# Attention probabilities turned by DVE in 32x32 blocks instead of by PE, and a product with V in four 32-row groups of the PE array

## The reference

```python
scale = DIM_HEAD ** (-0.5)                      # 16 heads of 64
xn = layer_norm(x, ln_g, ln_b)                  # x: (32, 112, 256)
cn = layer_norm(context, cln_g, cln_b)          # context: (32, 375, 256)
q = (xn @ Wq).reshape(b, n, HEADS, DIM_HEAD).transpose(0, 2, 1, 3) * scale
k, v = jnp.split(cn @ Wkv, 2, axis=-1)          # one k and one v for all heads
sim = jnp.einsum('bhid,bjd->bhij', q, k) + mask[:, None, :, :]
attn = jax.nn.softmax(sim, axis=-1)
out = jnp.einsum('bhij,bjd->bhid', attn, v)
out = out.transpose(0, 2, 1, 3).reshape(b, n, INNER) @ Wout
val, gate = jnp.split(xn @ W1, 2, axis=-1)
out = out + jax.nn.silu(gate) * val @ W2
```

## Time and profile before

| | |
|---|---|
| median of 3 runs | 1851.41 us (1844.26 to 1853.59) |
| span of the profiled execution, first to last instruction | 1848.1 us |
| PE matmul busy | 1761.8 us, 95% of the span |
| DVE busy | 1310.7 us, 71% |
| ACT busy | 918.7 us, 50% |
| POOL busy | 420.3 us, 23% |
| groups 1 to 6, each | 149.7 us |

### The profile page before, as it was taken

How to read it: one execution, slowest core, us unless ns; L and a number is a source line. 1 busy time by engine, 2 the same in 40 slices (tenths; PEclk the granted TensorE clock), 3 DMA queues, 4 the chain that set the end, 5 groups by cost and what they waited for, 6 DMA issues and landing times.

```text
span 1848.1 us, 27947 instructions
## 1 busy us (share of the span) xinstructions
PE 1761.8 (95%) x9224; PEld 1020.1 (55%) x9224; DVE 1310.7 (71%) x3971; ACT 918.7 (50%) x2262; POOL 420.3 (23%) x569
## 2 busy tenths in 40 slices
PE   4579999999999998999999999999999999999997
PEld 2356676766767544455545554544555554555466
DVE  6878988988976588476667648747747666765744
ACT  3444553553541465456545545645645654654542
POOL 4868677777872001000000000000000000000000
PEclk8689999999999999999999999999999999999999
DMA  4000000000013343232222222323223322232200
GB/s 132 11 11 11 21 21 11 31 21 27 6 39 111 95 138 103 55 79 73 73 67 72 76 71 65 81 57 80 66 64 79 75 70 68 72 82 58 54 19 21
DMA packets 102318, 109.22 MB, mean 59 GB/s; under 512 B 38592, under 2 KB 95872, under 8 KB 101280
## 3 DMA queue, kind: packets, MB, share of 16 engines
q1 hardware_dynamic: 101712, 106.99, 21.7%
q10 hardware_dynamic: 464, 0.46, 0.1%
HBM read 96.92 MB, written 7.42 MB: 56 GB/s over the span
## 4 chain that ended last, share of the span: by engine, by line
PE 86%; DVE 8%; ACT 2%; DMA 2%; issue 1%; POOL 1%; DVEq 0%; POOLq 0%; ACTq 0%
PE ps L1530 20%; PE ps L1485 9%; PE ps L1492 9%; PE ps L1523 9%; PE ps L1508 8%; PE ps L314 5%; PE ps L440 4%; PE ps L387 4%; PE ps L427 4%; PE ps L405 3%; PE ps L1590 2%; DVE m_u L727 2%; PE ps L373 2%; PE ps L1584 1%; PE ps L1628 1%
## 5 line engine op out<-in xcount | busy, mean ns | idle before, releaser
L1867 DVE CUSTOM_DVE_ANT_0 x_pr<-ps,x_mk 128x375 f32<-128x375 f32 x448 | 227.6, 545 | 306.1 <-issue 238.9
L1739 ACT ACTIVATE x_pT<-ps 125x384 f32<-125x384 f32 x448 | 195.5, 489 | 269.8 <-PE ps L1492 269.2
L1745 ACT ACTIVATE x_pr<-x_pr,x_mx 128x375 f32<-128x375 f32 x448 | 268.2, 608 | 30.4 <-DVE x_mx L1867 30.4
L1492 PEld LDWEIGHTS ps<-ident,x_pr 128*125 128x125 f32 x1344 | 164.5, 187 | 130.9 <-issue 95.7
L1492 PE MATMUL ps<-ident,x_pr 128*125 128x128 f32 x1344 | 205.7, 289 | 2.5 <-DVE x_pr L1876 2.5
L1530 PE MATMUL ps<-x_xn,x_w 128*128 128x448 f32 x512 | 205.7, 543 | 2.1 <-DVE x_ff L1927 2.1
L1485 PE MATMUL ps<-x_kT,x_qT 64*128 64x375 f32 x896 | 202.6, 529 | 4.1 <-DVE x_mx L1867 4.1
L1876 DVE TENSOR_SCALAR x_pr<-x_pr,x_rc 128x375 f32<-128x375 f32 x448 | 170.9, 424 | 8.0
L1508 PE MATMUL ps<-x_pT,x_va 125*64 125x512 f32 (+1 forms) x768 | 158.4, 548 | 0.6 <-ACT x_pT L1739 0.6
L314 PE MATMUL ps<-m_xa,w_in 128*128 128x448 f32 x352 | 148.2, 568 | 6.2 <-ACT m_xa L532 6.2
L1485 PEld LDWEIGHTS ps<-x_kT,x_qT 64*128 64x128 f32 x896 | 67.7, 185 | 126.3 <-issue 114.4
(11 more groups left out here) (195 smaller groups left out, 2867.3 us busy)
## 6 DMA issues: line engine op xcount, KB each, us to landing
x_mk<-in_mask SPq DMA_DIRECT2D x224, 187.5 KB, 2.4
x_cx<-in_context SPq DMA_DIRECT2D x32, 375.0 KB
x_cT<-in_context_turned SPq DMA_DIRECT2D x32, 375.0 KB, 3.3
x_rb<-context_roots SPq DMA_DIRECT2D x32, 187.5 KB, 4.9
m_Rd<-bc_roots SPq DMA_DIRECT2D x8, 448.0 KB, 3.6
x_mixed<-m_x SPq DMA_DIRECT2D x8, 448.0 KB, 4.0
X<-x_mixed SPq DMA_DIRECT2D x8, 448.0 KB, 4.9
m_X<-in_x SPq DMA_DIRECT2D x7, 448.0 KB, 4.0
```

The costliest lines, as they stand in the source:

```text
L1492: last = pe.transpose(bank(2 + e)[0:JP, t * ROWS:(t + 1) * ROWS], pr[:, 2 * (p % SLOT) + e, t * JP:(t + 1) * JP], ident[:, :])
L1739: act.activation(pT[:, 2 * NV * (batch(p) % 2) + 2 * (p % NP % NV) + e, :, :].rearrange("p t s -> p (t s)"), bank(2 + e)[0:JP, 0:JT * ROWS ...
L1745: act.activation(pr[:, k, :], pr[:, k, :], ACT.Exp, scale=-1.0, bias=mx[:, k:k + 1], accum_out=sums[:, k:k + 1]).then_inc(h_e.sem, 1)
L1867: dve.tensor_tensor_reduce(pr[:, k + e, :], bank(e)[:, 0:J], mk[:, p % SLOT, :], -1.0, 3.0e38, ALU.add, ALU.min, mx[:, k + e:k + e + 1]).t ...
```

## The change

The probabilities are no longer turned by PE. ACT now multiplies them by the reciprocal (`scaled`, in the step after `exps`), DVE turns them within blocks of 32x32 (`turn`, one instruction of 128x384 for each e) into a ring of nine places (`blocks`), and DVE's reciprocal (`divide`) moves to the end of its own step. ACT's two `copies` out of PSUM go. Each block row of 32 partitions then holds other query rows for the same 32 keys, so the product with V is done in four groups of 32 rows of the array at once, each with its own copy of V (`va` has V four times; still eight DMAs for a batch, each with four times as many pieces of 128 bytes) and into its own PSUM bank (2, 3, 4 and 5). A batch takes 12 key blocks x 4 row groups x 2 values of e = 96 matmuls of 224 columns, in two halves at steps 1 and 2 of the next batch, between the slots X and Y, and four copies in `heads_out` at step 3. Since four banks go to this product, the filler pieces have two seats, banks 6 and 7, in place of three, and the table of pieces is laid out anew. The table also decides when the norms run. Some buffers are shared (`so` in place of `so`, `x2` and `fs`), and the last group's end uses other banks.

```diff
-NV = 4
-NB = 2
 SLOT = 4
-MISC = (6, 7, 5)
+MISC = (6, 7)
 SEATS = len(MISC)
 XB = 2
-RESULT, TOKENS, TOKENS_FIRST, FINAL = (10, 11, 12), (20, 21, 22), (16, 17, 20), {STEPS - 2: (0,), STEPS - 1: (1, 2)}
+RESULT, TOKENS, TOKENS_FIRST, FINAL = (11, 12, 13), (17, 20, 23), (16, 17, 20), {STEPS - 2: (0,), STEPS - 1: (1, 2)}
+BLK = 32
+RB = ROWS // BLK
+JC = 12
+JW = JC * BLK
+AHEAD_BY = 2
+RING = NP + AHEAD_BY
+V_AT, V_TAKEN = (1, 2), 3
+V_BANKS = (2, 3, 4, 5)
+UP_BANKS = (0, 2, 3, 4)
 CONTEXT = (0, 1, 4)
-VPARTS = DH // 32 * (ROWS // 32)
+VPARTS = RB * DH // BLK
...
-    for c in range(KD):
-        for n in range(4):
-            at[4 * c + n + (1 if c or n >= 2 else 0), "Y"].append(("out", c, n))
+    for n in range(QUERIES, KA):
+        at[n - QUERIES, "X"].append(("query", n))
+    for n, p in enumerate(OUT_AT):
+        at[p, "Y"].append(("out", n // KA, n % KA))
     for n, s in enumerate("XY"):
-        at[9, s].append(("back", n))
+        at[11, s].append(("back", n))
+        at[17, s].append(("ftoken", n))
+        at[25 + n, "Y"].append(("down", n))
+        at[25, s].append(("token", n))
     for f in range(KH):
-        at[W1_AT + f, "X"].append(("gate", f))
-        at[W1_AT + f, "Y"].append(("value", f))
-    for n, s in enumerate("XY"):
-        at[18, s].append(("ftoken", n))
-        at[24, s].append(("token", n))
-        at[25, s].append(("down", n))
+        at[GATE_AT[f], "X"].append(("gate", f))
+        at[VALUE_AT[f], "Y"].append(("value", f))
     for n in range(KH):
-        at[20 + n // 2, "XY"[n % 2]].append(("up", n))
+        at[UP_AT[n], "Y"].append(("up", n))
     for b in range(GB):
         at[(b - 1) % GB * NP + NP - 2, "X"].insert(0, ("kv", b))
-    at[STEPS - 1, "Y"] += [("query", n) for n in range(QUERIES)]
-    for n in range(QUERIES, KA):
-        at[n - QUERIES, "X"].append(("query", n))
+    for n in range(QUERIES):
+        at[STEPS - 1 - (n == 0), "Y"].append(("query", n))
...
+OUT_AT = (0, 0, 3, 3, 4, 5, 5, 6, 6, 7, 7, 7, 8, 9, 10, 10)
+GATE_AT, VALUE_AT = (11, 12, 13, 14, 15, 17, 19, 20), (11, 12, 13, 14, 16, 17, 19, 20)
+UP_AT = (18, 18, 21, 21, 22, 23, 24, 24)
...
         return int(piece[0] == "value")
     if piece[0] == "out":
-        return 2
-    if piece[0] == "kv":
-        return 2 if piece[1] != 1 else 0
+        return 1 - piece[1]
+    if piece[0] == "kv" or piece[0] == "query" and piece[1] >= QUERIES:
+        return 0
     return piece[-1] % 2
...
-    pT = sb("x_pT", [JP, 2 * 2 * NV, JT, ROWS])
+    blocks = sb("x_blk", [ROWS, RING, 2, JC, BLK])
...
+    def tile_of(p):
+
+        b, n = divmod(p, NP)
+        return (n + NP - AHEAD_BY * (b % 2)) % NP
+
+    def place_of(p):
+
+        return tile_of(p) + AHEAD_BY * (p // NP % 2)
...
-        def values_in(i, b):
+        def values(i, b):
+
             sp.wait_ge(c_t.sem, c_t.value(i, b + 1))
-            hold(sp, h_o, i, NB * (b - 1))
-            for k in range(DH // 32):
-                for q in range(ROWS // 32):
-                    n = min(32, JP - 32 * q)
-                    sp.dma_start(va[32 * q:32 * q + n, b % 2, :, 32 * k:32 * k + 32], vT[32 * k:32 * k + n, :, 32 * q:32 * q + 32]).then_inc(l_va[b % 2].sem, 16)
+            hold(sp, h_o, i, b - 1)
+            for a in range(RB):
+                for k in range(DH // BLK):
+                    sp.dma_start(va[BLK * a:BLK * a + BLK, b % 2, :, BLK * k:BLK * k + BLK],
+                                 vT[BLK * k:BLK * k + BLK, :].rearrange("p (c x) -> p c x", x=BLK)).then_inc(l_va[b % 2].sem, 16)
...
-        def turn(i, p):
...
-        def times_v(i, p):
...
+        def times_v(i, b, part):
+
+            if part == 0:
                 pe.wait_ge(l_va[b % 2].sem, l_va[b % 2].value(i, VPARTS * 16 * (b // 2 + 1)))
-                hold(pe, o_c, i, 2 * b)
-            else:
-                pe.wait_ge(o_c.sem, o_c.value(i, 2 * b + 1))
-            n, k = r % NV + 1, 2 * NV * (batch(p) % 2)
-            for t in range(JT):
-                for e in range(2):
-                    last = pe.matmul(bank(4)[DH * e:DH * e + DH, 0:n * ROWS], va[:, b % 2, t, :], pT[:, k + e:k + 2 * n:2, t, :],
-                                     start=(t == 0), stop=(t == JT - 1))
-            last.then_inc(h_o.sem, 1)
+                pe.wait_ge(h_t.sem, h_t.value(i, 2 * NP * (b + 1)))
+                hold(pe, o_c, i, RB * b)
+            places = slice(AHEAD_BY * (b % 2), AHEAD_BY * (b % 2) + NP)
+            for c in range(JC // len(V_AT) * part, JC // len(V_AT) * (part + 1)):
+                for a in range(RB):
+                    rows = slice(BLK * a, BLK * a + BLK)
+                    for e in range(2):
+                        last = pe.matmul(bank(V_BANKS[a])[DH * e:DH * e + DH, 0:NP * BLK], va[rows, b % 2, c, :], blocks[rows, places, e, c, :],
+                                         start=(c == 0), stop=(c == JC - 1))
+            if part == len(V_AT) - 1:
+                last.then_inc(h_o.sem, 1)
...
-                if p == 0 and not first:
-                    turn(*back(it, p, 2))
                 scores(it, p)
                 if first and p == 6:
                     result_taken(LAST)
-                if p >= 3 or not first:
-                    times_v(*back(it, p, 3))
-                if p >= 2 or (p == 1 and not first):
-                    turn(*back(it, p, 2))
                 parts(it, p, "X", first, last)
+                if p % NP in V_AT and (p >= NP or not first):
+                    i, at = back(it, p, NP)
+                    times_v(i, at // NP, V_AT.index(p % NP))
                 parts(it, p, "Y", first, last)
...
+        def scaled(i, p):
+            k = 2 * (p % SLOT)
+            act.wait_ge(h_r.sem, h_r.value(i, p + 1))
+            for e in range(2):
+                act.activation(pr[:, k + e, 0:J], pr[:, k + e, 0:J], ACT.Copy, scale=rc[:, k + e:k + e + 1]).then_inc(h_n.sem, 1)
+
+        def heads_out(i, b):
+
+            if b == 0 and i >= 2:
+                filled(act, i - 1, ("out", KD - 1, KA - 1))
+            act.wait_ge(h_o.sem, h_o.value(i, b + 1))
+            for a in range(RB):
+                act.activation(OT[i % 2][:, b, :].rearrange("p (r a x) -> p r a x", a=RB, x=BLK)[:, :, a, :],
+                               bank(V_BANKS[a])[:, 0:NP * BLK].rearrange("p (r x) -> p r x", x=BLK), ACT.Copy).then_inc(o_c.sem, 1)
...
-                if p >= 3 or not first:
-                    heads_out(*back(it, p, 3))
-                if p >= 2 or not first:
-                    copies(*back(it, p, 2))
+                if p >= 1 or not first:
+                    scaled(*back(it, p, 1))
                 exps(it, p)
+                if p % NP == V_TAKEN and (p >= NP or not first):
+                    i, at = back(it, p, NP)
+                    heads_out(i, at // NP)
...
+        def turn(i, p):
+
+            if p % NP == AHEAD_BY:
+                hold(dve, h_o, i, p // NP)
             for e in range(2):
-                dve.tensor_scalar(pr[:, k + e, :], pr[:, k + e, :], rc[:, k + e:k + e + 1], None, ALU.mult).then_inc(h_n.sem, 1)
+                dve.wait_ge(h_n.sem, h_n.value(i, 2 * p + e + 1))
+                dve.transpose(blocks[:, place_of(p), e, :, :].rearrange("p c x -> p (c x)"), pr[:, 2 * (p % SLOT) + e, :]).then_inc(h_t.sem, 1)
...
-                    divide(*back(it, p, 1))
+                    turn(*back(it, p, 1))
                 b, r = divmod(p, NP)
                 if r in CONTEXT and not (last and b == GB - 1) and not (first and p == 0):
                     context_norm(it, (b + 1) % GB, CONTEXT.index(r))
...
+                divide(it, p)
```

More of the change, by code:

```diff
@@ L1109 @@
 MLP_DOWN, MLP_SUM, MLP_ROOT, MLP_NORM = (0, 1, 2, 3), (2, 4), 10, 12
-BEHIND = ([("out", c, n) for c in range(KD) for n in range(4)] + [("back", 0), ("back", 1), ("ftoken", 0), ("ftoken", 1)]
+BEHIND = ([("out", c, n) for c in range(KD) for n in range(KA)] + [("back", 0), ("back", 1), ("ftoken", 0), ("ftoken", 1)]
           + [("up", n) for n in range(KH)] + [("down", 0), ("down", 1)] + [("query", n) for n in range(QUERIES, KA)])
@@ L1129, in __init__ @@
     def __init__(self):
-        body, opening = ([x for p in range(STEPS) for s in "XY" for x in at[p, s] if x[0] != "out" or x[2] == 3] for at in (AT, AT_FIRST))
+        body, opening = ([x for p in range(STEPS) for s in "XY" for x in at[p, s] if x[0] != "out" or x[2] == KA - 1] for at in (AT, AT_FIRST))
         self.start, _ = self.places(STARTED)
@@ L1399, in group @@
             for p in range(STEPS):
-                if p == 12 and not first and not last:
+                if p == 13 and not first and not last:
                     sp.wait_ge(o_s.sem, o_s.value(it, 0))
@@ L1658, in end_up @@
                     pe.wait_ge(h_m.sem, h_m.value(NG - 1, U))
-                if h == 0 and n == 2:
-                    pe.wait_ge(h_c.sem, h_c.value(NG - 1, U))
-                if KH * h + n >= 4:
-                    pe.wait_ge(t_hq.sem, t_hq.value(h, n - 3))
+                if h == 0 and n == 1:
```

(41 more changed lines are left out.)

157 lines of the change are left out of this document (68 added, 89 removed).

## The result

The changed kernel takes 1921.2 us (median; 1920.1 to 1922.4), the kernel before 1851.8 beside it: 1.0388 times as long, 95% interval 1.0366 to 1.0410. The forecast was 1897, with 1862 to 1960 as its range.

What follows compares the result with a forecast made beforehand. PE's gapless list was taken as the bound in groups 1 to 7: 17.3 us saved against 23.6 of waits, 6.3 more a group. With 1848 + 46 = 1894 of span and 3.3 for the median, 1897 us; range 1862 to 1960.

Steps and rivals of the forecast that it cites:

- PE's own list: PE's work in a steady group, without waits: from 149.7 to 132.4 us, 17.3 less.
- fewer than eight together: Rival in times_v: four passes together give 2030 us, longer waves 1935, two some 2300; chance 0.13, longer waves included.
- DVE and ACT: Their lists in a group: DVE 9 us more, 108 of 132; ACT near 87; neither the bound by its sum.
- The rival of 0.9 us a transpose: DVE's transposes on 128 partitions cost 0.9 us: 161 a group, 1936 us; chance 0.05 together with dearer SP.
- that of SP: Rival: issuing the eight DMAs grows with their pieces, over 1950 us; chance 0.05 together with dearer transposes.
- The waits for seats: PE waits until ACT or DVE has read the piece before in bank 6 or 7: 23.6 us a group.
- the walk: The three engines' lists carried through the 28 steps with forecast durations, giving the waits, 23.6 us a group.
- the clock: Rival: PE's clock falls once a group behind its waits, at some 2 us, +15; no chance of its own, nothing taken.
- the idle stretch of the earlier trace: In group 0 PE worked 0.63 of 5.2 us; the granted clock was then 0.50 for the next 5.2.
- The sum: Six periods +38, group 7 +6, its end +2, group 0 0: span 1894 us, plus 3.3 for the median, 1897.

Runs made afterwards that it cites:

- two seats alone: The kernel before with two banks (6 and 7) for the filler pieces in place of three, all else unchanged: 1899.5 us, 1.0261 times before.
- the old table: The changed kernel with the old kernel's table of pieces and norm steps, in two seats: 1871.1 us, 1.011 times before.
- the run with PE kept busy: The changed kernel with 15 matmuls more in a group, on constant data, ahead of the pieces that wait longest: 1892.8 us, 1.023 times before.
- the new table: The changed kernel with other places, seats and norm steps for the same pieces: 1767.1 us, 0.9554 times before.
- the best version: The changed kernel with another table, group 0's pieces spread and GpSimd's multiplication in eight instructions: 1760.5 us, 0.9499 times before.

## Why the prediction was right, and what was off

- **PE's own list.** Forecast 132.4 us a group. Measured: 139.84 busy less half of the 12.8 us that PE was busy at half clock, 133.4. A half of `times_v` was to take 2.47 and takes 2.46. Rival "fewer than eight together": alone, 96 passes of 224 columns would take 96 x 0.188 = 18 us at the 0.84 ns of the earlier trace rows, so 7.3 run together. The Trainium skill ("TensorE: Matmul & The Clock Gate", Part 3) has 3.07 times for four row groups; this trace, with two column halves as well, shows nearly the full eight, and the measurement decides.
- **DVE and ACT.** A pair of transposes takes 1.04 (forecast 1.06), two `scaled` 1.11 by their record and 1.02 from the first's start to ACT's next instruction (forecast 0.51 each, 1.02), four head copies 1.06 (1.2). Half the transposes left out moved a group by 1.2 us. The rival of 0.9 us a transpose is out, and so is that of SP: 5.23 us to issue eight DMAs.
- **The waits for seats.** They came at the forecast places. In the order of the steps 11, 11, 12, 14, 15, 17, 17, 19, 21, 25 and 26, forecast and (group 5): 3.4 (3.1), 1.7 (1.5), 4.0 (3.4), 1.5 (1.4), 2.1 (1.6), 3.7 (3.2), 0.9 (0.6), 2.0 (2.0), 0.8 (0.8), 2.8 (2.4), 0.6 (0.6). Sum 23.6 (20.6): the walk was too dear by 3, spread over the larger ones. That seats are the cause is shown three ways: two seats alone cost the old kernel 7.3 us a group, clock included; another table takes 24 off the new one; the old table takes 7 to 10 off it. The two tables move the norms as well, and step 12 shows why that counts: the norm's stage makes ACT, and with it the emptying of the seat, late.
- **The term that was mis-sized: the clock.** The prediction took nothing for it, since the waits were shorter than the idle stretch of the earlier trace rows, and put 15 us in all on a fall a group. There are three falls a group, 13.65 us at half clock, in which PE worked for 12.8: 6.4 us lost, or 6.0 by the run with PE kept busy (160.5 - 154.5), which over six groups is 38 us. The group: 156.0 + 1.0 (list) - 3.0 (waits) + 6.4 (clock) = 160.4. That the forecast was not further off is in part luck: the waits forecast 3.0 too dear hid nearly half of what the clock took.
- **The sum.** The six periods were to be 38 us longer and are 66 (964.0 - 898.4). Group 0, taken as unchanged, is 2.4 shorter; group 7 and the end were to cost 6 + 2 and cost 7.6; the median lies 1.8 above the span and not 3.3. That makes +28 - 2 - 0 - 2 = 24, the distance from 1897 to 1921. Group 1 takes 163.1, 2.6 more than the steady ones, and has more of the same: five falls, 20.5 us at half clock in place of 13.65, worth 3.4. Group 2, at 158.9, has three short ones, 10.2 us.

## What to carry to other kernels

Where an engine runs gapless, what it gains by shedding work depends on who frees its buffers: count two users of one buffer within one step before counting the work saved, and lay the order of the pieces out anew when a buffer goes. Price a wait of TensorE together with the clock that it loses: here a wait of 3.9 us cost 7.3. And try the layout before giving up the idea: the same instructions in another order took this change from 3.9% slower to 4.5% faster.

## What the runs showed of the hardware

- **The clock falls behind short waits.** One wait of 3.86 us in 150 us of gapless work was followed by 6.83 us at a granted clock of 0.50, 1.2 GHz; in the changed kernel waits of 3.42, 3.15 and 2.39 us each stood beside a fall, and one of 3.07 (step 11) did not. In the first case the clock fell 3.15 us into the wait, at 1446.22, and PE worked again from 1446.93; in group 1 the same wait cost a fall of 3.41 us only. Filling the waits with matmuls that nobody needs made the kernel 28 us faster.
- **It falls without a wait, too.** With the row groups one after the other PE had no gap in the 9.00 and 13.40 us of the rows above, and yet the clock was at half for 3.8 us of the first (9.00 at a mean of 0.79) and through all of the second. It fell at 1421.39, and PE had had no gap since 1414.50, where it came out of a wait of 1.55. In the changed kernel a half of `times_v` lasts 2.46 us only, with eight tiles at work, and the new table's steady groups have no fall. Whether it is the fewer tiles at work or the length of the stretch was not told apart.
- **GpSimd holds up DVE.** While GpSimd's one `tensor_scalar` on 128x2048 elements ran (5.37 us), a DVE instruction on 112x4 elements took 3.51 us in place of 0.16 (DVE and GpSimd in order of time, changed kernel):

```profile
697.73 0.16 DVE L77 SCALAR_TENSOR_TENSOR x_st<-x_st 112x4 f32<-112x4 f32 x1
...
697.79 5.37 POOL L1487 TENSOR_SCALAR x_w<-x_w 128x2048 f32<-128x2048 f32 x1 [104.62 <-DMA x_wo<-in_x_wo]
697.93 3.51 DVE L73 TENSOR_TENSOR x_st<-x_st 112x4 f32<-112x4 f32 x1
...
701.48 0.16 DVE L75 SCALAR_TENSOR_TENSOR x_st<-x_st 112x4 f32<-112x4 f32 x1
```

The hold ended at 701.44, 3.65 us after GpSimd's start and 1.7 before the end of its record. The run with PE kept busy has the same 3.65, and there a later `tensor_tensor` took 0.16 at 705.01, while GpSimd's record runs to 706.30. So in these traces what comes in the last part is not held. A DVE `tensor_scalar` on 112x4 elements was held to the end (4.35 us, up to 704.27 against 704.25, new table alone).

With eight instructions in its place (the best version; 6.55 us in all) the same DVE instruction takes 0.39 each time, and the ones on L75 and L77 0.16:

```profile
698.01 0.39 DVE L73 TENSOR_TENSOR x_st<-x_st 112x4 f32<-112x4 f32 x1
698.43 0.16 DVE L75 SCALAR_TENSOR_TENSOR x_st<-x_st 112x4 f32<-112x4 f32 x1
```

Each L73 starts 0.02 us behind the start of one of GpSimd's eight, and L75 and L77 fall in what is left of it after the hold. That they are not held there says nothing of their kind. Where a `scalar_tensor_tensor` does start early in a GpSimd instruction, in the mixer of the changed kernel, it is held too, 0.51 us in place of 0.18:

```profile
42.68 0.18 DVE L75 SCALAR_TENSOR_TENSOR m_st<-m_st 112x20 f32<-112x20 f32 x1
...
43.81 0.57 POOL L967 TENSOR_TENSOR m_tg<-m_G,m_D 128x112 f32<-128x112 f32 x1
43.91 0.51 DVE L75 SCALAR_TENSOR_TENSOR m_st<-m_st 112x20 f32<-112x20 f32 x1
```

The Trainium skill ("SBUF — State Buffer", "SBUF: two separate sides") has it that the two engines share a pair of ports, which whoever is first holds for its whole instruction against a DVE operation with two inputs in SBUF. The traces agree that both kinds of operation with two inputs are held. They do not show the whole instruction: against `tensor_tensor` the hold lasts 3.65 of the 5.37 us of GpSimd's record. The spans of GpSimd in a trace are rough, but in the new table's run the record ends together with the held `tensor_scalar`, so the difference stays open.
